# Cross-attention and FFN on one core: narrow value matmuls in pairs, and roundings directly behind the exponentials

## The reference, cut to what matters

```
x: [32, 64, 512]   ctx: [32, 64, 512]          # float32
q = proj(layernorm(x), Wq, bq); k, v = proj(ctx, Wk, bk), proj(ctx, Wv, bv)   # -> [b, h=16, s, d=8, m=4]
q, k, v = interfere(q), interfere(k), interfere(v)    # x + 0.1 amp * einsum('bhsdi,hij->bhsdj', x, interference)
scores  = einsum('bhqdm,bhkdm->bhqkm', q, k) / sqrt(8)
weights = softmax(scores, over k)
o       = einsum('bhqkm,bhkdm->bhqdm', weights, v)
x  = x + o.reshape(b, s, 512) @ Wo.T + bo
h  = silu(layernorm(x) @ w_gate) * (layernorm(x) @ w_up)     # 4-bit weights, [512, 2 * 1376], dequantized by groups
y  = x + h @ w_down                                          # 4-bit weights, [1376, 512]
```

## Time and profile before

| | us |
|---|---|
| median of 3 runs | 935.25 (934.78 to 936.47) |
| profiled execution | 938.67 |
| its span, first to last instruction | 936.9 |
| TensorE busy (matmul) | 752.7 (80%) |
| VectorE busy | 632.9 (68%) |
| ScalarE busy | 421.4 (45%) |
| GpSimd busy | 323.7 (35%) |
| mean granted TensorE clock | 0.893 of full speed |

### The profile page before, as it was taken

One profiled execution on the slowest core, in us unless ns is written; L12 is line 12 of the kernel. 1 busy time (PEld: TensorE's weight loads), 2 busy tenths in 40 slices (PEclk: granted clock), 3 DMA queues, 4 the chain that ended last, 5 costly groups with the idle time before them and its releaser, 6 DMA issues.

```text
span 936.9 us, 22385 instructions
## 1 busy us (share of the span) xinstructions
PE 752.7 (80%) x8929; PEld 528.8 (56%) x8929; DVE 632.9 (68%) x1475; ACT 421.4 (45%) x774; POOL 323.7 (35%) x290
## 2 busy tenths in 40 slices
PE   6314567666997898789888988898889889988798
PEld 6203323322676477647764766476647655765485
DVE  6987776676567767765776587657865786657621
ACT  2326466655454345525452645264426443553220
POOL 6653155345133313331342135213521353043211
PEclk9657655555999999999999999999999999989999
DMA  8900222220100020002000200110011000100000
GB/s 245 295 3 1 76 62 61 73 71 31 47 2 1 14 81 2 2 24 69 2 2 24 69 2 2 46 47 2 2 47 47 2 1 24 24 2 2 23 1 23
DMA packets 20697, 36.49 MB, mean 39 GB/s; under 512 B 3374, under 2 KB 7602, under 8 KB 20592
## 3 DMA queue, kind: packets, MB, share of 16 engines
q1 hardware_dynamic: 20604, 35.08, 12.8%
HBM read 26.56 MB, written 4.19 MB: 33 GB/s over the span
## 4 chain that ended last, share of the span: by engine, by line
PE 50%; DVE 31%; issue 8%; ACT 7%; DMA 2%; SPq 1%; DVEq 0%; ACTq 0%; POOL 0%
PE bank L511 12%; PE bank L482 9%; PE bank L492 9%; PE bank L526 7%; DVE nmf L1153 6%; DVE osum L1113 4%; PE bank L644 3%; DVE nm L1163 2%; DVE arena L714 2%; PE bank L624 2%; DVE nrest L1165 2%; DVE rinv L1114 2%; ACT arena L849 2%; DMA arena<-in_L_xattn_Wo 2%; PE bank L460 1%
## 5 line engine op out<-in xcount | busy, mean ns | idle before, releaser
L511 PE MATMUL bank<-arena,WGU 128*128 128x256 f16 (+1 forms) x2112 | 254.7, 275 | 1.4 <-DVE arena L714 1.4
L511 PEld LDWEIGHTS bank<-arena,WGU 128*128 128x128 f16 (+1 forms) x2112 | 204.6, 101 | 28.0 <-DVE arena L714 1.8
L1370 POOL TENSOR_TENSOR arena<-arena 128x512 f16<-128x512 f32 x128 | 145.2, 1163 | 177.9 <-ACT arena L856 177.8
L1357 POOL TENSOR_TENSOR arena<-arena 128x512 f16<-128x512 f32 (+1 forms) x48 | 51.7, 1077 | 232.3 <-ACT arena L834 232.3
L526 PE MATMUL bank<-WD,arena 128*128 128x512 f16 (+1 forms) x528 | 126.9, 379 | 1.6 <-DVE arena L1129 1.6
L482 PE MATMUL bank<-arena,WT 128*128 128x256 f16 x768 | 92.0, 281 | 39.1 <-DVE arena L714 38.0
L849 ACT ACTIVATE arena<-bank,small 128x512 f32<-128x512 f32 x128 | 79.4, 687 | 63.6 <-PE bank L650 63.6
L482 PEld LDWEIGHTS bank<-arena,WT 128*128 128x128 f16 x768 | 76.9, 101 | 54.7 <-issue 42.0
L1103 DVE SCALAR_TENSOR_TENSOR arena<-arena,small 128x512 f16<-128x512 f32 x64 | 45.3, 749 | 72.2 <-ACT arena L818 72.2
L1153 DVE TENSOR_REDUCE nmf<-bank 128x8 f32<-128x512 f32 x128 | 81.4, 681 | 15.0 <-PE bank L624 15.0
L492 PE MATMUL bank<-WT,arena 128*128 128x512 f16 x384 | 89.4, 388 | 1.8 <-DVE arena L712 1.8
(11 more groups left out here) (162 smaller groups left out, 1063.3 us busy)
## 6 DMA issues: line engine op xcount, KB each, us to landing
arena<-in_L_ffn_qweight_gu SPq DMA_DIRECT2D x8, 688.0 KB, 5.2
arena<-arena SPq DMA_DIRECT2D x32, 132.0 KB, 2.4
WT<-in_ctx SPq DMA_DIRECT2D x8, 512.0 KB, 15.2
arena<-in_ctx SPq DMA_DIRECT2D x8, 512.0 KB, 3.6
arena<-in_x SPq DMA_DIRECT2D x8, 512.0 KB, 3.6
out_y<-arena SPq DMA_DIRECT2D x16, 256.0 KB, 2.1
arena<-in_L_ffn_qweight_down SPq DMA_DIRECT2D x10, 256.0 KB, 3.5
arena<-in_L_xattn_Wk SPq DMA_DIRECT2D x1, 1024.0 KB, 6.0
```

Of the source, the lines that this page charges most:

```text
L511: mm = e.matmul(pb[0:m, i * TOK:(i + 1) * TOK], WGU[:, sp, kb, half * INTER + fb * P:half * INTER + fb * P + m], x2T[:, mp, kb, :], start= ...
L1370: e.tensor_tensor(phl[:, a, 1, :], pring[:, a, :], phl[:, a, 0, :], ALU.subtract).then_inc(S["p_lo"], 1)
```

## The change

- **Value product.** A row of V becomes 36 wide: 16 high columns, two of ones, 16 low, two zeros. The product is three matmuls of 2 x 17 = 34 columns that add up in PSUM (exponential high x value high, low x high, high x low; the fourth half product is left out). Two slots form a pair p in bank JB[0]: 24 matmuls. A pair waits for the output of the pair before it.
- **Output.** VectorE takes one reciprocal of 16 columns for a pair and two products straight from PSUM, one for each 64 partitions. The reductions are gone. The columns of the output buffer have another order, so Wo is permuted with 32 copies of 64 columns, before 16 of 128.
- **Order in a batch.** Four FFN slots, before six: scores, slot 0, pair 2b-2, slot 1, pair 2b-1, turning of the maxima, transposes, slot 2, turned scores, slot 3. ScalarE makes the copy of the turned maxima (before VectorE), and works exponential, rounding, exponential, rounding ... for all four slots before FFN slot 3. GpSimd works the four remainders before its slot 3.
- **Banks.** The transposes of the attention (x, ctx, o) all go to JB[1]; each waits for the low half of the one before it, and the turned scores no longer wait for them.
- **Budget.** PRE, EACH and TAIL change, and with 22 slots, before 30, so do the ticks of chunk 0.

```diff
-VROW = 2 * 2 * DK + 1
+VROW = 36
+VCOLS = 2 * DK + 1
-PRE, EACH, TAIL = (24, 44), (14, 12, 10, 10, 11, 11), (16, 12, 12, 16)
+PRE, EACH, TAIL = (16, 26), (20, 22, 8, 24), (16, 16, 10, 16)
@@ t_bank
-            return {"x2T0": GB, "x2T1": UB, "oT0": AB[2], "oT1": AB[0]}.get(name, AB[1])
+            return {"x2T0": GB, "x2T1": UB}.get(name, JB[1])
@@ pe_extras, for each name
+                e.wait_ge(S["t_lo"], t_at(c, name) - 1)
@@ pe_chunk
                 pe_scores(e, c, b)
                 ffn_slice(slot[0])
                 if b:
-                    pe_values(e, c, 4 * b - 4)
+                    pe_values(e, c, 2 * b - 2)
                 ffn_slice(slot[1])
                 if b:
-                    pe_values(e, c, 4 * b - 3)
+                    pe_values(e, c, 2 * b - 1)
+                pe_turn_max(e, c, b)
+                pe_extras(e, c, b)
                 ffn_slice(slot[2])
-                pe_turn_max(e, c, b)
-                names = pe_extras(e, c, b)
+                pe_scores_turned(e, c, b)
                 ffn_slice(slot[3])
-                if names:
-                    e.wait_ge(S["t_lo"], t_at(c, names[-1]))
-                pe_scores_turned(e, c, b)
-                ffn_slice(slot[4])
...
@@ pe_values, pair p
+            for s in (2 * p, 2 * p + 1):
+                b, a = s // 4, s % 4
+                e.wait_ge(S["p_lo"], SLOTS * c + s + 1)
+                for i in range(KB):
+                    at = (KB * (s % 2) + i) * 2 * VCOLS
+                    for n, (part, v0) in enumerate(((0, 0), (1, 0), (0, VROW // 2))):
+                        mm = e.matmul(JB[0][:, at:at + 2 * VCOLS], phl[:, a, part, i * P:(i + 1) * P],
+                                      vv[:, b, :, 4 * i + a, v0:v0 + VCOLS], start=(n == 0), stop=(n == 2))
@@ act_chunk
-                act_slot(e, c, slot[2], first)
+                act_copy_max(e, c, b)
                 for name in EXTRAS[b]:
                     if name in (T_LAST if last else T_ORDER):
                         act_hi(e, c, name)
+                act_slot(e, c, slot[2], first)
+                for s in range(4 * b, 4 * b + 4):
+                    act_exp(e, c, s)
+                    act_p_hi(e, c, s)
                 act_slot(e, c, slot[3], first)
...
@@ dve_setup
-                                ins = e.tensor_copy(wop[g][:, (2 * hh + j) * P:(2 * hh + j + 1) * P].rearrange("p (h q d) -> p h q d", h=8, q=2),
-                                                    ap(wraw[3][:, g], 0, P, 256 * hh + j, [(32, 8), (2, 2), (4, 8)]))
+                                for a in range(2):
+                                    at = (4 * hh + 2 * j + a) * 64
+                                    ins = e.tensor_copy(wop[g][:, at:at + 64].rearrange("p (i q d) -> p i q d", i=KB, q=2),
+                                                        ap(wraw[3][:, g], 0, P, 64 * hh + 32 * a + j, [(128, KB), (2, 2), (4, 8)]))
@@ dve_o, pair p
+            e.reciprocal(rinv[:, k, :], ap(JB[0], 0, P, VCOLS - 1, [(VCOLS, 16)])).then_inc(S["o_step"], 1)
...
+                ins = e.tensor_tensor(ap(obuf, 64 * j, 64, 256 * b + 64 * a, [(16, 8), (8, 2), (1, DK)]),
+                                      ap(JB[0], 64 * j, 64, DK * j, [(2 * VCOLS, 8), (VCOLS, 2), (1, DK)]),
+                                      ap(rinv, 64 * j, 64, 16 * k, [(2, 8), (1, 2), (0, DK)]), ALU.mult)
@@ pool_chunk
-                for k in slot[:4]:
+                for k in slot[:3]:
                     pool_slot(e, c, k, first)
...
+                for s in range(4 * b, 4 * b + 4):
+                    pool_p_lo(e, c, s)
+                pool_slot(e, c, slot[3], first)
```

More of the change, by code:

```diff
@@ L46 @@
 UNITS = (FB + 1) // 2
-VROW = 2 * 2 * DK + 1
+VROW = 36
+VCOLS = 2 * DK + 1
+PAIR = 2 * KB * 2 * VCOLS
 LN_SCALE = 64.0
@@ L463, in pe_extras @@
         def pe_extras(e, c, b):
-            names = [n for n in EXTRAS[b] if n in (T_LAST if is_last(c) else T_ORDER)]
-            for name in names:
+            for name in EXTRAS[b]:
+                if name not in (T_LAST if is_last(c) else T_ORDER):
+                    continue
+                e.wait_ge(S["t_lo"], t_at(c, name) - 1)
                 if name[0] == "o":
@@ L1223, in dve_chunk @@
                 if b:
-                    dve_o(e, c, 4 * b - 4)
+                    dve_o(e, c, 2 * b - 2)
                 dve_slot(e, c, slot[1], first)
                 if b:
-                    dve_o(e, c, 4 * b - 3)
-                dve_slot(e, c, slot[2], first)
-                dve_copy_max(e, c, b)
+                    dve_o(e, c, 2 * b - 1)
                 for name in EXTRAS[b]:
@@ L1232, in dve_chunk @@
                         dve_lo(e, c, name)
-                dve_slot(e, c, slot[3], first)
+                dve_slot(e, c, slot[2], first)
                 if b == 0 and not last:
@@ L1380, in pool_chunk @@
                     pool_ln(e, "x", c + 1)
-                pool_slot(e, c, slot[4], first)
-                pool_p_lo(e, c, 4 * b)
-                pool_slot(e, c, slot[5], first)
-                for a in range(1, 4):
-                    pool_p_lo(e, c, 4 * b + a)
+                for s in range(4 * b, 4 * b + 4):
+                    pool_p_lo(e, c, s)
+                pool_slot(e, c, slot[3], first)
             for k in AT_TAIL:
```

96 lines of the change are left out of this document (31 added, 65 removed).

## The result

The changed kernel takes **960.7 us** (median of 4 runs, 958.7 to 961.8), the kernel before on the same chip 935.9: ratio 1.026, 95% interval 1.024 to 1.028. It is slower by 24.9 us, where 4.8 were forecast, and outside the range of 925 to 950. The profiled execution took 958.72 us (span 957.0), the fastest of its runs, against 938.67 before: 20.05 us more. These 20 us can be placed. Of the other 5, 2.8 are the kernel before, whose traced execution was over its median: its mean granted clock was 0.893, and of its later runs those at 0.893 and 0.894 took 938.8 to 939.2 us, those at 0.896 and more 937.9 and less. The last 2, by which the kernel after ran under its median, stay open.

What follows compares the result with a forecast made beforehand. It took hand-overs between engines to bound the kernel. Setup +2.5, chunk 0 +4.5, six chunks -0.6 and the last -1.6 gave +4.8 us on the 935.25 median: 940.0 us, range 925 to 950.

Steps and rivals of the forecast that it cites:

- rival 4: TensorE's clock: waits of 2.0 us once a batch are like those of now; a fall got no chance of its own.
- the hand-over of an FFN bank: Last slot of batches 2 and 3: TensorE waits for a bank ScalarE frees behind the roundings, +0.9 and +1.2 us.
- exponentials: Middle chunk: next batch's scores wait 2.0 us for the fourth exponential, three times a chunk, +5.9 us.
- masks of Q: Ahead of batch 0: less FFN work covers the masking of Q behind its projection, +1.6 us of wait.
- second transposition: Batch 3: two transposes share a bank, the second waits for the first's remainder; +1.5 us, 0.6 in chunk 0.
- first value pair: Middle chunk: the first value pair of a batch waits behind the product, +0.2 us.
- The value matmuls: TensorE: 12 matmuls of 34 columns a slot for 8 of 66, at 26 ns each, +1.0 us a chunk.
- rival 1: Narrow value matmuls stream at 16 ns, saving 13 us: 927 us; chance 0.30 with its like.
- The four blocks: Chunk 0: exponentials and roundings at one stretch ahead of a tick's ScalarE step, +3.3 us a batch, +11.6 in all.
- the stall of the split: Chunk 0: maxima and slow split hold VectorE's tick step three times by 3 us; 1 us left, -6.0 us.
- Rival 2: Dequantization chain decides: chunk 0's blocks at full 5.1 us and slow split, +12, copies +6: 951 us; chance 0.10.
- VectorE's share: Output work for two slots falls from 2.0 to 0.8 us, freeing some 9 us a chunk, off the path except in the tail.

Runs made afterwards that it cites:

- e1: Changed kernel with ScalarE's four roundings of a batch moved behind its four exponentials: 955.4 us, ratio 1.019 to the kernel before.
- e6: Changed kernel, only chunk 0 altered: ScalarE and GpSimd do a dequantization step behind each exponential and rounding: 958.9 us.
- e2: Changed kernel with the last FFN slot's ScalarE work put between the four exponentials and the four roundings: 965.2 us.
- e4: Kernel before with only the new value matmuls and the products straight from PSUM, without reductions: 923.2 us.
- e17: e9 with slots of 14, 13, 13, 6, 11, 11 units (903.8 us), plus two needless TensorE waits in every batch except in chunk 0: 940.5 us.
- e9: e4 plus values in pairs in one bank, transposes in the other, 32 copies; engine order, six slots and budget as before: 915.3 us.
- e13: e9 with ScalarE's copy of the maxima (911.1 us), plus the block, both pairs ahead of the turned scores, six re-budgeted slots: 1015.6 us.
- e15: e9 with slots of 14, 13, 13, 6, 11, 11 units (903.8 us), plus one needless TensorE wait in batch 2 except in chunk 0: 914.0 us.

## Why the prediction was wrong

**The step that failed first: rival 4.** "I give a fall of the clock no chance of its own" left out 5.8 us of the middle chunks' 10.5, and the fall in chunk 1 is its whole +1.6 (-0.1 forecast). Its reason was that a middle chunk before had waits of up to 2 us at clock 1.00. That was true of the waits as they lay there. The change put the hand-over of an FFN bank, for which I counted +1.2, right behind the wait for the exponential with the scores alone between. Both were in my sum, as two prices; I did not lay them side by side. The kernel before could have told me that a fall has a chance, though not where: its last chunk is at 0.96 in the earlier trace rows, for a fall (834 us) behind waits of 1.31 and 1.45 us with ten FFN units between. Each of its middle chunks has longer waits ahead of the same two instructions, with 1.8 us of work between them for 1.3, and none has a fall:

```profile
558.28 0.23 PE L634 MATMUL bank<-ident,nm 128*128 128x128 bf16 x1 [1.32 <-DVE nm L1169]
...
558.79 1.26 PE L511 MATMUL bank<-arena,WGU 128*128 128x256 f16 x10
561.80 0.35 PE L644 MATMUL bank<-arena 32*128 32x128 f16 x12 [1.75 <-DVE arena L714]
```

**The middle chunk.** Without a fall it is 0.94 us longer, forecast -0.1. Its parts, in idle slots (listed plus 0.16 each, plus 0.05 for the hand-over behind the scores): exponentials 5.8 (5.9 forecast), masks of Q 1.86 (1.6), second transposition 1.64 (1.5), hand-overs 1.2 and 0.96 (1.2 and 0.9), first value pair 0.4 (0.2), and 0.4 that the view calls issue, which I had struck out with the waits removed. They add to 12.2, just what was removed, 0.9 over my 11.3. The value matmuls cost +0.8, forecast +1.0: 24 in 0.60 us in the timeline above, 25 ns each for my 26, and 16 took 0.50 before. By the Trainium skill, "TensorE: Matmul & The Clock Gate", section "Wait — 56ns, not 53.3ns?", they come no closer than about 25 ns; the trace agrees. So rival 1 falls. The small terms that were low make 1 us, five times 4.7. With no fall the forecast would still have been low by that, and by chunk 0.

**Chunk 0**, +8.0 for +4.5. The four blocks cost 3.3 us each, as forecast (L445 waits 4.83 for 1.50). The term that failed is the stall of the split, -6.0: three waits of 3.2 to 3.5 us for 4.1 to 4.5 are -3.1, though the split is quick now. At 137.85 VectorE still needs 4.1 us until L1077: 1.3 for the maxima, 0.9 for the split, 0.9 for the output, and 0.93 for the conversion L1066, which takes 0.48 in its median; in the three places it takes 0.93, 1.38 and 0.93 us, each time with GpSimd's L1318 beside it. The wait of the second transposition is 1.5 for 0.6. Rival 2 had the direction; its causes, blocks at their full 5.1 us and a slow split, did not come. Neither of the other orders of ScalarE mends chunk 0: 132.0 us in e1, 132.6 in e6, 143 in e2.

**Setup**, +1.4 for +2.5: the 32 copies lasted 13.3 us from first to last, the 16 before 11.7. That is +1.5, where I had +0.9 for the copies and +1.6 for more of GpSimd's work; no row tells the two apart. **The last chunk**, -0.3 for -1.6: I struck out a middle chunk's waits there, but it had 8.2 us of them listed for 10.1, and the small terms are low as above. It isn't its fall, as the kernel before has one twice as long in it (6.8 us). **The FFN behind it**, -1.1 for nothing: its listed waits are the same, and the fall in it lasts 3.4 us for 6.8. That is luck.

**VectorE's share** I called off the path. e4 shows that it was on it: 13.5 us came from this part, though TensorE pays 0.8 a chunk for it. In the sum this did not show, because all waits at the split and the turned scores were struck out whatever removed them.

**The steps of the change**, in medians: values -13.5, pairs with banks and copies -7.9, the maxima's copy -4.2, the block +104.5, the four slots with their bank -54.9, in all +24. The step called the block has the places of the values and six slots' units in it too, and a third of it in a middle chunk is the clock. The prediction priced the block against 24 units of cover and was right for the final schedule, falls apart; that without its slots it costs 104 is a price no row of before shows.

**Open**: what decides whether waits bring a fall. The same two brought one in some chunks and none in others (above). Waits of 1.32 and 1.75 us with 1.8 us of work between brought none in the middle chunks before, and 1.31 and 1.45 with 1.3 us between brought one in the last chunk; e17 has more of them and none. That it takes both is shown for batch 3 of the kernel after alone.

## What to carry to other kernels

When several waits of a sum end up next to each other on TensorE, or one grows (2.04 us brought a fall in two chunks of e1), price them as a place, not one by one: look in the timeline at how little work is left between them, and give the clock's fall (1.6 us each here) a chance of its own. When two schedules are compared, compare TensorE's busy time too: where it differs for the same matmuls, part of the gain or loss is the clock. In this kernel ScalarE's chain was cheaper cut in two around an FFN hand-over than in one block: with the value products where the block needs them it cost 104 us, and only a new budget of cover brought half back. Moving four units of cover a batch from behind one wait to ahead of another was worth 11.5 us, nearly as much as the new value product (13.5).

## What the runs showed of the hardware

The granted clock of TensorE fell from 1.00 to 0.50 (2.4 to 1.2 GHz) for 3.4 us behind waits of 1.73 and 1.14 us (e9: 0.28 and 1.50 us), in one chunk and not in the next of identical work: in e9 in every second one (from 311, 488 and 666 us). It fell behind single waits of 2.04 and 2.36 us (e1), and in or behind those of 2.44 to 4.08 us (e13). One inserted wait of 1.7 us a chunk (e15), or six of 0.9 to 1.4 (e17), brought none in a middle chunk, and neither did 1.32 and 1.75 us with 1.8 us of work between (before). Matmuls of 34 columns and full height came 25 ns apart. Copies of 128x64 elements took 0.207 us where those of 128x128 took 0.264: half the size is not half the time.
